# GNN and expert layer on one core: accumulating scatters wait by expert, GpSimd's loop is unrolled, index columns are used in place

## The reference

```
xn     = layernorm(x)
logits = xn @ Wg + bg + bias                       # 3125 x 8
w      = softmax(top2(logits)); combine = w at the two experts, 0 elsewhere
h      = relu(xn @ W1[e] + b1[e])                  # 256 -> 512
y      = h @ W2[e] + b2[e]                         # 512 -> 256
out    = x + sum over e of y[e] * combine[e]
```

## Time and profile before

| | |
|---|---|
| median of 3 runs | 1861.9 us (1859.88 to 1865.39) |
| span of the profiled execution, first to last instruction | 1864.8 us |
| PE, DVE, ACT, POOL busy in the span | 85%, 39%, 19%, 12% |
| first gather of the expert loop | 1558.60 us |
| last scatter of the expert loop starts | 1854.33 us |
| TensorE's granted clock from 1596 to 1838 us | 1.00 |

### The profile page before, as it was taken

The page is one execution under the profiler, slowest core; times in us unless marked ns, Lnnn a source line. Parts: engine busy times, 40 slices in busy tenths (PEclk is TensorE's granted clock), DMA queues, the critical chain, the costliest instruction groups (busy, mean ns, idle before and its releaser), DMA issues.

```text
span 1864.8 us, 26392 instructions
## 1 busy us (share of the span) xinstructions
PE 1586.2 (85%) x9010; PEld 937.9 (50%) x9011; DVE 719.5 (39%) x1899; ACT 362.7 (19%) x822; POOL 218.8 (12%) x281
## 2 busy tenths in 40 slices
PE   1288887678999989998999989998999757989884
PEld 1266765344778545453545354444444425555553
DVE  4699995565444323012311122012201553322221
ACT  0054554000000132002300140013000321323231
POOL 1011110000000000000000000000000004565553
PEclk8699998999997799998999989999999778999998
DMA  3000001330000000000000000000002352333332
GB/s 89 10 2 1 1 2 61 115 122 28 1 1 1 12 13 1 0 1 13 1 1 1 1 12 1 1 1 12 1 1 84 114 173 67 52 51 51 53 51 33
DMA packets 49875, 57.63 MB, mean 31 GB/s; under 512 B 13967, under 2 KB 41249, under 8 KB 49504
## 3 DMA queue, kind: packets, MB, share of 16 engines
q1 hardware_dynamic: 39008, 41.35, 6.9%
q0 software_dynamic: 10752, 14.69, 4.9%
HBM read 42.04 MB, written 13.99 MB: 30 GB/s over the span
## 4 chain that ended last, share of the span: by engine, by line
PE 57%; DMA 14%; DVE 11%; issue 9%; POOL 5%; DVEq 2%; ACT 1%; POOLq 1%; SPq 0%
PE bank L625 35%; PE bank L706 12%; DMA out_rows<-ytb,nowS 6%; DMA slrow<-sl_dram 5%; DVE cnt L1365 5%; PE bank L1676 4%; DMA xin<-in_x 3%; POOL out_rows L857 2%; POOL xtb L848 1%; PE bank L614 1%; PE bank L709 1%; PE bank L1604 1%; DVE ohS L1362 1%; PE bank L1085 1%; DVE ohT L1420 1%
## 5 line engine op out<-in xcount | busy, mean ns | idle before, releaser
L625 PE MATMUL bank<-at,m 125*128 125x500 fp8e4 (+1 forms) x3500 | 712.6, 361 | 1.3 <-DVE m L593 1.3
L625 PEld LDWEIGHTS bank<-at,m 125*128 125x128 f16 x3500 | 328.3, 101 | 329.1 <-issue 28.3
L1604 PE MATMUL bank<-cnt,ohS 128*128 128x313 bf16 x900 | 137.9, 302 | 85.1 <-DVE cnt L1365 81.7
L634 DVE TENSOR_TENSOR aggT<-bank,dinvB 128x500 f32<-128x500 f32 (+1 forms) x70 | 42.1, 620 | 346.3 <-PE bank L625 335.2
L1365 DVE TENSOR_SCALAR cnt<-iotaK,keyE,powE 128x626 bf16<-128x626 int16 x450 | 164.9, 430 | 0.0
L1604 PEld LDWEIGHTS bank<-cnt,ohS 128*128 128x128 bf16 x900 | 107.0, 127 | 110.8 <-DVE cnt L1365 93.1
L837 POOL TENSOR_TENSOR idJ<-idJ,wts 125x1400 f32<-125x1400 f32 x2 | 8.0, 4006 | 1260.6 <-DVE idJ L1003 1260.6
L797 ACT ACTIVATE hT<-bank,prm 128x500 f32<-128x500 f32 (+1 forms) x70 | 40.5, 630 | 593.2 <-PE bank L709 593.2
L1134 PE MATMUL bank<-w2s,h1T 128*128 x448 | 110.6, 390 | 20.5 <-issue 19.1
L706 PE MATMUL bank<-hT,wcur 128*128 128x500 f32 (+1 forms) x280 | 124.5, 567 | 0.0
L759 DVE BATCH_NORM_STATS2 zst<-hT 128x6 f32<-128x500 f32 (+1 forms) x70 | 40.2, 616 | 198.8 <-ACT hT L797 198.8
(11 more groups left out here) (292 smaller groups left out, 1338.1 us busy)
## 6 DMA issues: line engine op xcount, KB each, us to landing
slrow<-sl_dram SPq DMA_DIRECT2D x32, 406.2 KB
w1s<-in_L_ffn_W SPq DMA_DIRECT2D x1, 4096.0 KB, 14.3
w2s<-in_L_ffn_W SPq DMA_DIRECT2D x1, 4096.0 KB, 20.2
xin<-in_x SPq DMA_DIRECT2D x1, 3125.0 KB
x<-in_x SPq DMA_DIRECT2D x1, 3125.0 KB
out_rows<-x SPq DMA_DIRECT2D x1, 3125.0 KB
xn_dram<-xn SPq DMA_DIRECT2D x1, 3125.0 KB
wraw<-in_L_gnn_mlp_w SPq DMA_DIRECT2D x5, 512.0 KB, 3.9
```

The lines of the kernel that those rows point to most:

```text
L625: last = pe.matmul(bank[banks[g]][:, 0:w], m[:, s, k, h * 128:(h + 1) * 128], at[:, s, a:a + w], start=s == 0 and k == 0, stop=s == NT - 1 ...
L1604: last = pe.matmul(bank[GB * (t % 2) + b][:, 0:GC], ohS[r][:, :, j], cnt1[r][:, j, b * GC:(b + 1) * GC], start=r == 0 and j == 0, stop=r = ...
```

## The change

Four things change together.

- **Waits.** A scatter no longer waits for the one before it. VectorE computes `ts`, one plus the number of tiles of the experts that end before tile j. GpSimd reads `ts[j]` into a register and waits on a new semaphore `s_done` for it: all tiles of preceding experts have landed. Scatters of one expert may be in flight together. Each of the four buffers has its own `s_acc`, and SyncE, idle by then, passes their completions on in order of the tiles as counts of `s_done`. VectorE waits on `s_done` before it writes a buffer again.
- **Index columns.** The indirect DMAs take the columns of `rowG` and `rowS` themselves; `nowG`, `nowS`, their copies and the waits for them are gone.
- **Loop.** GpSimd's steps are written out, all 56.
- **VectorE** has three more instructions ahead of the loop, for `ts`.

```diff
+        tsF = r("tsF", [1, J], F32)
+        ts = r("ts", [1, J], I32)
...
-        s_acc = sem("s_acc")
+        s_acc = [sem(f"s_acc{k}") for k in range(XB)]
+        s_done = sem("s_done")
...
+            sp.sem_inc(s_done, 1)
+            for j in range(J):
+                sp.wait_ge(s_acc[j % XB], 16 * (j // XB + 1))
+                sp.sem_inc(s_done, 1)
...
-            def gather(j, k):
-
-                pool.tensor_copy(nowG[:, k:k + 1], rowG[:, bass.ds(j, 1)]).then_inc(s_nowG, 1)
-                pool.wait_ge(s_nowG, j + 1)
+            def gather(j):
 
                 pool.sem_inc(s_apart, 1)
-                pool.indirect_dma_start(xtb[:, k, :], None, xn_dram[:, :], bass.IndirectOffsetOnAxis(ap=nowG[:, k:k + 1], axis=0)).then_inc(s_xt[k], 16)
-
-            def accumulate(j, k):
-
-
-                pool.tensor_copy(nowS[:, k:k + 1], rowS[:, bass.ds(j, 1)]).then_inc(s_nowS, 1)
-                pool.wait_ge(s_nowS, j + 1)
+                pool.indirect_dma_start(xtb[:, j % XB, :], None, xn_dram[:, :], bass.IndirectOffsetOnAxis(ap=rowG[:, j:j + 1], axis=0)).then_inc(s_xt[j % XB], 16)
+
+            def accumulate(j):
+
+                before = pool.value_load(ts[0:1, j:j + 1], min_val=1, max_val=J + 1)
+                pool.wait_ge(s_done, before)
                 pool.wait_ge(s_yb, j + 1)
                 pool.sem_inc(s_apart, 1)
-                pool.indirect_dma_start(out[:, :], bass.IndirectOffsetOnAxis(ap=nowS[:, k:k + 1], axis=0), ytb[:, k, :], None,
-                                        compute_op=ALU.add).then_inc(s_acc, 16)
...
-            group(0, True, False)
-            with pool.Fori(1, J // XB - 1) as g:
-                group(g, False, False)
-            group(J // XB - 1, False, True)
-            pool.wait_ge(s_acc, 16 * J)
+            pool.wait_ge(s_slot, 1)
+            for j in range(J):
+                if j + XB < J:
+                    pool.wait_ge(s_xtT, j + 1)
+                    gather(j + XB)
+                accumulate(j)
+            pool.wait_ge(s_done, J + 1)
...
             step(dve.tensor_reduce(teF[:, :], cmpJ[:, :, :], axis=XYZ, op=ALU.add))
+            step(dve.tensor_tensor(cmpJ[:, :, :], cmpJ[:, :, :], nte[0:1, 1, :].unsqueeze(1).to_broadcast([1, J, NE]), ALU.mult))
+            step(dve.tensor_reduce(tsF[:, :], cmpJ[:, :, :], axis=XYZ, op=ALU.add))
+            step(dve.tensor_scalar(ts[:, :], tsF[:, :], 1.0, None, ALU.add))
...
-                    dve.wait_ge(s_acc, free)
+                    dve.wait_ge(s_done, free)
```

More of the change, by code:

```diff
@@ L278, in gnn_ffn_program @@
         wS = r("wS", [128, J], F32)
-        nowG = r("nowG", [128, XB], I32)
-        nowS = r("nowS", [128, XB], I32)
         wts = r("wts", [P, 3, NT], F32)
@@ L438, in gnn_ffn_program @@
         s_yb = sem("s_yb")
-        s_nowG = sem("s_nowG")
-        s_nowS = sem("s_nowS")
-        s_acc = sem("s_acc")
+        s_acc = [sem(f"s_acc{k}") for k in range(XB)]
+        s_done = sem("s_done")
         block = ctx.enter_context(nc.Block())
@@ L871, in experts_pool @@
-            for k in range(XB):
-                gather(k, k)
+                pool.indirect_dma_start(out[:, :], bass.IndirectOffsetOnAxis(ap=rowS[:, j:j + 1], axis=0), ytb[:, j % XB, :], None,
+                                        compute_op=ALU.add).then_inc(s_acc[j % XB], 16)
+            for j in range(XB):
+                gather(j)
             pool.wait_ge(s_res, 32)
             pool.wait_ge(s_tab, 2)
-            group(0, True, False)
-            with pool.Fori(1, J // XB - 1) as g:
-                group(g, False, False)
@@ L1038, in group @@
                         hidden(j + 1, (k + 1) % 2)
-                    result(j, k % 2, k, None if first else 16 * (XB * before + k + 1))
+                    result(j, k % 2, k, None if first else XB * before + k + 2)
             hidden(0, 0)
```

## The result

The changed kernel takes 1811.6 us, the median of four runs (1806.69 to 1815.75), against 1863.6 (1859.88 to 1865.39) for the kernel before, on the same chip. The ratio is 0.972, with a 95% interval of 0.970 to 0.975. On another chip, with five runs, it was 0.972 again (0.970 to 0.974). The forecast was 1810.

What follows compares the result with a forecast made beforehand. GpSimd's step of about 5 us was taken as the bound, TensorE's 4.10 next. Steps 46.9 + tail 7.1 - VectorE 1.5 + copy 0.2 - hop 0.1 = 52.6 us less than 1861.9: 1810 us, range 1804 to 1840.

Steps and rivals of the forecast that it cites:

- 217.3 in total: Expert loop: 53 TensorE steps at 4.10 us, in place of 264.19 us at 4.98.
- (a): Expert loop: TensorE paces it after the change at 4.10 us a step; 1810 us, chance 0.62.
- (b): Expert loop: GpSimd still paces, dispatch half hidden, 4.13 us a step; 1813 us, chance 0.17.
- the signs: Profile after: `up` every 4.10 us, gather 1.6 to 1.7 us after scatter, last scatter within 1 us of last `ytb`.
- Dispatch beside the engine's work: GpSimd's loop step: sequencer runs ahead, handing on DMAs while the engine works, so the step is under 4.10 us.
- (c): Expert loop: GpSimd still paces, no dispatch hidden, 4.92 us a step; 1849 us, chance 0.12.
- lower bound of 2.61 us: GpSimd's step if all dispatch lies beside the engine's work: scatter 1.60 plus gather 1.01 us.
- The load's price: GpSimd's register load between the DMAs: 0.505 us plus 0.182 of register work, 0.69 us together.
- At nothing: GpSimd's written-out loop alone costed at nothing; hardware-loop steps 2.4 us at most, beside the engine's scatter work.
- The changes of expert: Loop: at each change the scatter waits for a landing, 0.6 us late, fitting in some 3 us of slack.
- the tail: End of kernel: last scatter starts 0.88 us after the last `ytb` instead of 7.98, 7.1 us less; SyncE's hop 0.1 more.
- the sum: Whole kernel: steps 46.9, tail 7.1, VectorE -1.5, lost copy 0.2, SyncE's hop -0.1: 52.6 us less.

Runs made afterwards that it cites:

- the three extra loads: Changed kernel with three more unused loads of `ts` in each of GpSimd's steps: 1812.7 us, ratio 0.971 to the kernel before.
- the kernel with eight: Changed kernel with eight more unused loads of `ts` in each of GpSimd's steps: 1929.7 us, ratio 1.033 to the kernel before.
- the three with `te` and `ts` late and no 16 products: Changed kernel with `te` and `ts` instructions moved behind the first `ohR` pair, 1813.8 us; behind the last, 1810.1; that plus 5 unread TensorE matrix products, 1808.2.
- the kernel with products in two places: Changed kernel, `te` and `ts` behind the first `ohR` pair, plus unread TensorE matrix products: 16 before the index tables, 5 after: 1815.9 us, 0.973.

## Why the prediction was right

**What sets the pace.** Right. The prediction named GpSimd's step of 5.0 us as the bound and TensorE's own 4.10 as the next one. After the change the steps are 4.107 us, 0.4 us above 217.3 in total, and the chain holds TensorE alone. The saving on 53 steps is 46.5 us, predicted 46.9. Cases (a) and (b) are only 0.03 us a step apart (4.10 and 4.13), so the step itself could not tell them apart; the slack of 2.4 us and the three extra loads do. Two of the signs came out otherwise: the gather begins 1.90 us after a scatter and not 1.6 to 1.7, and the last scatter 1.46 us after the last `ytb` and not within 1.

**Dispatch beside the engine's work.** Right, and this was the disputed step on which cases (a), (b) and (c) parted. Two indirect DMAs behind one another are 0.30 us apart, in place of 0.79 with a copy and its semaphore between them; the prediction's lower bound of 2.61 us had put no gap there. The load is not on the path: three more change nothing.

**The load's price.** Mis-sized: 0.29 us for the load where 0.505 had been taken, and 0.55 in all where 0.69 had. The kernel before had only a single early load on GpSimd to go by. The Trainium skill's 600 ns ("DMA: Bandwidth & Descriptors", "Latency and other measured facts") is not what GpSimd's loads show here: 0.28 to 0.51 us over the 448 extra loads of the kernel with eight. The slack covered either.

**The role of the waits.** Wrong in its weighing. The prediction said that "what the new waits permit is therefore used little", because a scatter lands in 3.75 us and the step is 4.10. It had the right numbers beside it, 3.75 plus the hop plus 0.83 is 4.7, and used them for the change of expert alone. The kernel with the old wait shows that they hold in nearly every step: 4.74 us on average and 34 us more. It is the dispatch of one scatter that lies beside the landing of another, not the landings beside each other.

**The written-out loop.** "At nothing" was wrong for the kernel before: it alone gives 0.3%, 0.1 us a step. In the changed kernel GpSimd has 2.4 us of slack, so the 0.1 us should lie in it; a version with the hardware loop kept and the rest changed wasn't tried.

**The changes of expert.** Right. A scatter begins 0.83 us behind its `ytb` nearly everywhere, and 1.35 to 1.52 us behind it at tiles 11, 25, 32, 35, 39, 48, 52 and 55: eight times, 0.5 to 0.7 us each, predicted 0.6. These are the changes of expert: worked out from the inputs, the experts fill 11, 14, 7, 3, 4, 9, 4 and 3 tiles. TensorE's steps do not show them. The last change is at tile 55, which no later step hides: its scatter starts 1.46 us behind `ytb` (1795.17 to 1796.63), where I had put 0.88 and 0.1. This is most of what the tail fell short: from the last `up` to the end it is 20.2 us against 26.9, 6.6 less where 7.0 were predicted.

Tiles 37 and 44 are late as well, by 0.9 and 0.3 us, and not by a wait: GpSimd's semaphore step ends at once (tile 37: 1721.98, `ytb` at 1721.94), but from there to the sequencer's next own step it is 1.48 and 0.89 us, where it is 0.58 for the others. Tile 37 is late by the same 0.9 us in the second execution of the changed kernel and in four of the kernels made from it (three more loads, and the three with `te` and `ts` late and no 16 products), so it belongs to the program and not to chance. Why the dispatch is longer there stays open.

**VectorE and the start.** The three instructions cost 1.50 us, as computed, and the first gather comes 28.9 us after `cmpJ` starts against 27.7: 1.2 later, predicted 1.3. What the sum lacked is the first two steps. From the first gather to the third `up` it is 16.1 us against 15.1, since TensorE's granted clock was still 0.50 for most of the second `up` (until 1566.4 us), which took 3.37 us in place of 1.98. This is 0.9 us, and with the tail and the 0.4 us of the steps it makes up the 1.6 us between 52.6 and 51.0. It is not the change's: in the kernels with more loads the second `up` took 1.98 us and the stretch 14.0. How close 1810 and 1811.6 came is therefore luck in part: these first steps alone moved by 2 us.

**The part ahead of the loop.** In the twelve profiled executions (before, changed, and ten experiments) VectorE gets to the end of `slf` between 1524.1 and 1533.5 us, with none of its instructions changed up to there. The times of one kernel scatter by as much, 1806.7 to 1815.8 us for the changed one, and of the 5.7 us between its two profiled executions 5.5 lie ahead of this point. The cause stays open.

## What to carry to other kernels

Where two DMAs take turns on GpSimd, look for what must be finished between them: a copy made just ahead, or a landing waited for. Each puts the DMA's dispatch (0.8 us here) on the path; without them it lies beside the work. Two such waits that hold one step hide each other, so take both away or expect a quarter to a third of the gain. Find the next bound by the steps in which the queue is still full, and what it costs to get there by starts, not by busy shares. To judge a gain of a few us, look at more than one execution: the clock of the first steps and the landing of a store moved by 1 to 2 us here with nothing changed that bears on them.

## What the runs showed of the hardware

- VectorE's instructions with two SBUF operands took 2.94 and 2.20 us beside GpSimd's elementwise work, ending 0.47 to 0.49 us after GpSimd's instruction, and 0.61 us without it; a sum over one operand took 0.61 in both.
- After 4.2 us of idle time TensorE's granted clock was 0.50 of 2.4 GHz for the first `up` (3.77 us) and most of the second (3.37); in six of the ten executions without products the second ran at 1.00 (1.98 us). With five products in that time it was 1.00 for both. In the kernel with products in two places it was back at 0.50 after 4.49 us of idle time.
- A load of a register on GpSimd's queue takes 0.55 us with its register work and the gaps, and runs beside the engine's DMAs.
- A completion passed on by SyncE reached GpSimd's sequencer in 0.06 us.
- The sequencer took 0.58 us to hand on a scatter for nearly all tiles, and 1.48 and 0.89 us for two of them.
